# Two attentions: the first maxima turned earlier, later loads, and every row of maxima sent from ScalarE's queue

## The chip, the core and the metric

The program runs on one core of one Trainium2 chip. The metric is device time in microseconds (us) from the start to the end of one execution. The kernel before took 1791.27 us, the median of 3 runs (1789.46 to 1794.43). TensorE is called PE here, VectorE DVE, ScalarE ACT, GpSimd POOL, and SyncE, which only issues transfers, SP.

## The reference, cut to what matters

The program is a four-layer model on 16 sequences of 256 tokens, 128 features each. Each layer adds an attention-like part and an expert part to the residual. The change touches the attentions of the second layer (causal, called `att1`) and of the third (not causal, with low-rank additions, called `att2`). Both have 16 heads of 8 features:

```python
# layer 1 (causal)
q = proj(Wq, bq); k = proj(Wk, bk); v = proj(Wv, bv)            # 16 x 16 heads x 256 x 8
scores = einsum('bhqd,bhkd->bhqk', qc, k) * scale
scores = where(k_pos > q_pos, -inf, scores)
m = max(scores, axis=-1)
p = softmax(scores - m)
out = einsum('bhqk,bhkd->bhqd', p, v) @ Wo.T + bo
# layer 2 (not causal)
attn = softmax(einsum('bhnd,bhmd->bhnm', q, k) * ATTN_SCALE)
out = einsum('bhnm,bhmd->bhnd', attn, v) @ w_proj + b_proj
```

The time of these two attentions with the expert work that is set into the middle of each is about 720 to 1160 us and 1184 to 1530 us of the execution.

## The kernel before, in words

Both attentions are one function, `attention`. A projection stage (`projections`) computes all queries and keys, splits each into three bfloat16 parts and stores them to the chip's memory as `q_parts` and `k_parts`. Then a batch (one sequence) at a time is loaded back into one of four buffers of `qs` and `ks`, by 12 transfers that SP issues (`load_half` twice, L2149 and L2151). Load(b) means the 12 transfers of batch b. Batches 0 and 1 are loaded during the projection stage, batches 2 and 3 right after it.

The scores are computed twice. The first time (`maximum`, L2333) DVE takes the maximum of each row (`reduce`, L2515 and L2519). When the 8 pairs of heads of a batch are done, DVE splits the maxima into two bfloat16 parts (`split_maximum`), PE turns them (`turn_maximum`, L2416), ACT copies them to `mt` (L2497), and two small transfers (`top`, L2217, 8 KB each) put them as extra rows 48 and 49 into `qs`. Top(b) means the two transfers of batch b. The second time (`scores`, L2358) these rows subtract the maximum within the matmul, ACT takes the exponential (`exponent`, L2474), PE multiplies by the values (`values`, L2382), ACT copies the result out of the single bank O_BANK (`take_outputs`, L2479), and later steps turn, divide, turn back and project it.

The order is a loop over steps, `for step in steps`, written out for each engine: 8 steps to a batch, one for each pair of heads; the step within its batch is j. The maxima run LEAD = 12 steps ahead of the scores, so steps -12 to -1 hold only maxima. TURN = 5 places the turn and the copy of batch b + 1 in step j = 5 of batch b; project_values and the first `values` of the next pair of heads follow in step j = 6. On PE, the `values` of step 6 begin with a wait on `o_taken`, which counts the `take_outputs` of ACT; the one that it needs here is the first instruction of ACT in step 6, right behind the copy of the maxima in step 5:

```python
                    if k == 0:
                        ...
                        if gi >= 1:
                            pe.wait_ge(s.o_taken, gi)
```

Scores(8b) waits for top(b), maximum(8b) for load(b). At step MID (48 in att1, 32 in att2) all engines run the expert work (`job`) and then go on. In att2 that work has its own weights, `job.weights` (L2700 and L2695): six small transfers and two of 578 KB.

SP's order in the kernel before: the stores of the projection, load(2), then for each b from 0: top(b + 1), after b = 0 load(3), in att2 at b = 1 the weights, and load(b + 4) when the scores of batch b are done. Top(0) alone is issued by ACT.

Of the kernel before, what the change touches and what calls it, by code (L numbers as in the profile page):

```python
# [15 lines left out]
BATCH, T = 16, 256  # L16
# [2070 lines left out]
def attention(nc, g, title, prologue, project, wv, bv, wo, bo, q_parts, k_parts, causal, scale, moe=None, disp=None,  # L2087
              ybuf=None, r=None, dense=None):

    PAIRS = HEADS // 2  # L2090
    NP = BATCH * PAIRS
    NG = HEADS // 4
    LEAD = 12
# [6 lines left out]
    OT0, OT1, BACK, TURN, VALUES, OUT = 2, 3, 4, 5, 6, 7  # L2100
# [15 lines left out]
    with section(nc, title, *names, *PROJECT, "w_in", "filled", "ones_set", "consts", "biased", "qk_in0", "qk_in1", "qk_in2", "qk_in3",  # L2116
# [103 lines left out]
        with nc.Block() as block:  # L2220

            @block.sync
            def _(sp):
                def load(b):
                    if b % 2 == 0:
                        parts.chunk_stored(sp, b // 2)
                    for half in range(2):
                        load_half(sp, b, half)

                parts.sync(sp)  # L2230
                load(2)
                for b in range(BATCH - 1):
                    top(sp, b + 1)
                    if b == 0:
                        load(3)
                    if b == 1 and dense:
                        job.weights(sp)
                    if b + BUFS < BATCH:
                        sp.wait_ge(s.s_ready, (b + 1) * PAIRS)
                        load(b + BUFS)  # L2240
                    if moe and (b + 1) * PAIRS == MID:
                        job.first_tokens(sp)
                    if (moe or dense) and (b + 1) * PAIRS == MID:
                        job.sync(sp)
# [70 lines left out]
            def _(pe):  # L2315
# [121 lines left out]
                for step in steps:  # L2437
# [6 lines left out]
                        job.tensor(pe)  # L2444
                    if 0 <= step < NP:
                        scores(step)
                    if step + LEAD < NP:
                        maximum(step + LEAD)
                    if 2 <= step <= NP + 1:
# [2 lines left out]
                        turn_outputs(b - 1, j - OT0)  # L2452
                    if b >= 1 and j == BACK:
                        turn_back(b - 1)
                    if 0 <= b + 1 < BATCH and j == TURN:
                        turn_maximum(b + 1)
                    if 0 <= b + 1 < BATCH and j == VALUES:
                        project_values(b + 1)
# [4 lines left out]
            def _(act):  # L2463
# [17 lines left out]
                for step in steps:  # L2481
# [11 lines left out]
                    if 0 <= b + 1 < BATCH and j == TURN:  # L2493
                        act.wait_ge(s.turned_nm, b + 2)
                        if b >= 1:
                            act.wait_ge(mx_in[(b + 1) % 2], (b - 1) // 2 * 32 + 32)
                        nc.scalar.copy(mt[:, (b + 1) % 2, :], g.ps[0:4 * PAIRS, MISC, 0:T]).then_inc(s.mt_ready, 1)  # L2497
                        if b == -1:
                            top(act, 0)
                            parts.all_stored(act)  # L2500

            @block.vector
# [559 lines left out]
```

## Time and profile before

| what | value |
|---|---|
| median of 3 runs | 1791.27 us |
| time of the profiled execution | 1770.34 us |
| its span (first to last instruction) | 1768.5 us |
| PE, DVE, ACT, POOL busy | 84%, 71%, 53%, 45% of the span |
| granted clock of PE, mean | 0.927 |
| scores (L2358) of att1 | 760.57 us to 1153 us, with expert work from 843 to 1025 us |
| scores (L2358) of att2 | 1230.68 us to 1521 us, with expert work from 1294 to 1372 us |

The profiled execution took 1.84 us more than its span and was 20.9 us (1.2%) faster than the median. Busy shares are means over stages with different limits; what a stage is worth is read from its own stretch. In a row of windows the busy times stand in the order PE, PEld (weight loads), DVE, ACT, POOL, followed by PE's granted clock (1.00 is 2.4 GHz, 0.50 is 1.2 GHz), the busy share of the DMA engines and GB/s. In a timeline row the number in brackets is how long the engine sat idle before it and what ended that.

### The profile page before, as it was taken

What the parts mean: (1) busy time and instruction counts of PE and PEld (TensorE: products, weight loads), DVE (VectorE), ACT (ScalarE), POOL (GpSimd) and SP (SyncE); (2) the same over time, 40 slices, a digit from 0 to 9 for tenths busy, and PEclk for the clock granted to TensorE, in tenths of its full rate; (3) what the DMA queues carried; (4) which work ended last, traced back from release to release, by engine and by line L of the source; (5) the groups of instructions that cost most, each with busy time, mean ns of one, the idle gap of its engine ahead of it and who ended that gap; (6) DMA issues with size and microseconds to landing.
All of it is one profiled execution on the core that took longest, in us unless ns stands there. A gap on an engine that the chain in (4) does not pass through costs nothing. (4 is left out here: it accounts for less than half of the span.)

```text
span 1768.5 us, 31307 instructions
## 1 busy us (share of the span) xinstructions
PE 1479.8 (84%) x11180; PEld 921.1 (52%) x11180; DVE 1247.3 (71%) x2002; ACT 939.1 (53%) x1674; POOL 792.3 (45%) x722
## 2 busy tenths in 40 slices
PE   5993698898886877489799999954899999878997
PEld 5771244444342336256577766631345444566886
DVE  7745999999999987757355567668733899565335
ACT  1235578777775652546344456644554777533442
POOL 1477888778886743566144443124200000046341
PEclk9996899999999996779899999986899999779999
DMA  4522987877767946655322146207621342221223
GB/s 145 166 73 62 198 183 183 197 165 198 182 158 188 209 102 249 201 109 97 55 59 56 54 86 99 32 17 189 102 42 48 47 66 39 98 73 51 85 76 101
DMA packets 193559, 200.89 MB, mean 114 GB/s; under 512 B 22474, under 2 KB 142569, under 8 KB 193152
## 3 DMA queue, kind: packets, MB, share of 16 engines
q1 hardware_dynamic: 181816, 177.33, 42.9%
q0 software_dynamic: 11520, 21.52, 4.5%
q8 instruction: 93, 1.52, 0.4%
q14 instruction: 58, 0.48, 0.1%
q10 hardware_dynamic: 72, 0.03, 0.0%
HBM read 144.45 MB, written 57.48 MB: 114 GB/s over the span
## 5 line engine op out<-in xcount | busy, mean ns | idle before, releaser
L799 POOL TENSOR_TENSOR xn_t<-scan_b_rows,scan_du 128x1024 f32<-128x1024 f32 x128 | 303.9, 2381 | 94.2 <-DMA scan_b_rows<-states 62.5
L824 PE MATMUL banks<-scan_hc,ident 128*128 128x512 f32 x512 | 264.4, 629 | 77.4 <-DVE scan_hc L1006 76.7
L998 DVE TENSOR_TENSOR_SCAN banks<-banks,xn_t 128x1024 f32<-128x1024 f32 x128 | 293.1, 2290 | 27.9 <-POOL xn_t L799 17.7
L2474 ACT ACTIVATE att_pr<-banks 128x768 f32<-128x768 f32 (+1 forms) x256 | 234.4, 917 | 128.2 <-PE banks L2366 73.5
L824 PEld LDWEIGHTS banks<-scan_hc,ident 128*128 128x128 f32 x512 | 89.3, 194 | 212.5 <-DVE scan_hc L1006 147.1
L927 ACT ACTIVATE banks<-delta,scan_exp_centre,a_neg 128x510 f32<-128x510 f32 x256 | 189.3, 770 | 0.3
L2519 DVE TENSOR_REDUCE att_mb<-banks 128x4 f32<-128x1024 f32 x128 | 154.0, 1222 | 21.8 <-PE banks L2333 16.7
L2382 PE MATMUL banks<-att_pr,att_vx 128*32 128x256 f32 (+1 forms) x2048 | 155.7, 377 | 4.9 <-ACT att_ot L2479 3.3
L1006 DVE TENSOR_TENSOR scan_hc<-banks,scan_c_rows 128x1024 f32<-128x1024 f32 x128 | 156.5, 1223 | 3.8
L2515 DVE TENSOR_REDUCE att_mb<-banks 128x6 f32<-128x768 f32 x128 | 121.5, 956 | 46.8 <-PE banks L2340 45.7
L2333 PE MATMUL banks<-att_ks,att_qs 48*128 48x256 bf16 (+1 forms) x1024 | 112.4, 277 | 40.3 <-DMA att_ks<-k_parts 34.6
L1626 POOL IOTA xn_tok<- 128x32 int32 x1 | 0.2, 188 | 306.9 <-POOLq L78 306.9
L1442 POOL DMA_INDIRECT ybuf<-att_yo,att_xin x72 | 70.0, 972 | 126.0 <-DVE att_yo L1426 122.0
L2358 PE MATMUL banks<-att_qs,att_ks 50*128 50x256 bf16 (+1 forms) x1024 | 108.7, 269 | 15.3 <-DMA att_qs<-att_mt 12.7
L1342 PE MATMUL banks<-grouped_w,att_xt 128*128 x288 | 99.6, 469 | 0.4 <-DVE att_xt L1408 0.3
L925 ACT COPY banks<-zeros 128x4 f32<-128x4 f32 x128 | 20.8, 162 | 138.2 <-DVE scan_hc L1006 128.3
L1391 ACT ACTIVATE att_a<-banks 128x352 f32<-128x352 f32 x72 | 33.4, 464 | 107.0 <-PE banks L1342 107.0
L1061 POOL DMA_INDIRECT disp<-xn_tok,places x64 | 70.0, 1094 | 40.3 <-ACT u L545 24.9
L2298 POOL DMA_INDIRECT disp<-xn_tok,places x64 | 65.7, 1027 | 34.1 <-issue 12.4
L2333 PEld LDWEIGHTS banks<-att_ks,att_qs 48*128 48x128 bf16 x1024 | 48.7, 99 | 58.4 <-issue 24.7
L2358 PEld LDWEIGHTS banks<-att_qs,att_ks 50*128 50x128 bf16 x1024 | 39.8, 95 | 71.1 <-issue 39.9
L1408 DVE COPY att_xt<-banks 128x128 f32<-128x128 f32 x72 | 20.9, 292 | 76.3 <-PE banks L1332 76.3
(391 smaller groups left out, 3182.4 us busy)
## 6 DMA issues: line engine op xcount, KB each, us to landing
scan_b_rows<-states SPq DMA_DIRECT2D x128, 256.0 KB, 6.0
scan_c_rows<-states SPq DMA_DIRECT2D x128, 256.0 KB, 4.9
scan_ew<-f_packed SPq DMA_DIRECT2D x12, 578.0 KB, 6.0
q_parts<-att_p_parts SPq DMA_DIRECT2D x16, 384.0 KB, 3.6
k_parts<-att_p_parts SPq DMA_DIRECT2D x16, 384.0 KB, 5.6
att_qs<-q_parts SPq DMA_DIRECT2D x64, 96.0 KB
att_ks<-k_parts SPq DMA_DIRECT2D x64, 96.0 KB
disp<-blank_rows SPq DMA_DIRECT2D x1, 4680.0 KB, 15.1
```

Source lines behind the costliest of these rows:

```text
L799: nc.gpsimd.tensor_tensor(bu[:, q % AHEAD], b_rows[:, q % HELD, None, :].to_broadcast([P, DC, TT]), du[:, b % 2], ALU.mult).then_inc(s.bu_ ...
L824: nc.tensor.matmul(g.ps[:, Y0 + c, :], g.ident[:], hc[:, q % RING, c], start=False, stop=(q % DS == DS - 1)).then_inc(s.sum_done, 1)
L927: ins = nc.scalar.activation(inner(decays(q)[:, c]), inner(delta[:, c, span(b)]), ACT.Exp, scale=a_neg[:, c, n:n + 1], bias=exp_centre[:])
L998: v.tensor_tensor_scan(states, states, rows(bu[:, q % AHEAD]), 0.0, ALU.mult, ALU.add).then_inc(s.scan_done, 1)
L1006: v.tensor_tensor(hc[:, q % RING], decays(q), c_rows[:, q % HELD, None, :].to_broadcast([P, DC, TT]), ALU.mult).then_inc(s.hc_ready, 1)
L1342: ins = nc.tensor.matmul(g.ps[:, 4 * p + 1 + m, 0:H1], xt[:, p, :], rows(w13[:, bass.ds(expert[j], 1), m * H1:(m + 1) * H1]), start=True, ...
L2333: ins = nc.tensor.matmul(g.ps[:, 2 * m_slot(i) + half, lo:hi], qs[rows_of, p, j, q * P:(q + 1) * P], ks[rows_of, p, j, 0:hi - lo], start=T ...
L2358: ins = nc.tensor.matmul(g.ps[:, 2 * s_slot(i) + half, k * T:k * T + T - q0], ks[rows_of, p, j, k * P:(k + 1) * P], qs[rows_of, p, j, q0:T ...
L2382: ins = nc.tensor.matmul(g.ps[r * 32:(r + 1) * 32, O_BANK, q0:T], vx[:, b % 2, k, 4 * jg + r, :], pr[:, i % RING, half, k * T:k * T + T - q0],
L2474: nc.scalar.activation(pr[:, i % RING], g.ps[:, at:at + 2, 0:W], ACT.Exp, scale=scale).then_inc(s.p_ready, 1)
L2515: v.tensor_reduce(mb[:, b % 2, j, :].rearrange("p (g n) -> p g n", g=2), g.ps[:, at:at + 2, 0:W].rearrange("p g (n k) -> p g n k", k=P), A ...
L2519: v.tensor_reduce(mb[:, b % 2, j, :], g.ps[:, at:at + 2, :].rearrange("p g (n k) -> p (g n) k", k=T), AX_X, ALU.max).then_inc(s.m_taken, 1)
```

## The change

In `attention`, for both attentions: PE turns the maxima of batch 0 in step -4, before maximum(8), and no longer in step -3. SP waits until top(0) has landed before it issues load(2), and issues load(3) right behind it. The weights of att2's expert work are issued at b = 2, behind load(5), and no longer at b = 1, before load(5). Every top is now issued by ACT, directly after its copy of the maxima, where before SP issued all but the first.

```diff
                 parts.sync(sp)
+                sp.wait_ge(mx_in[0], 32)
                 load(2)
                 for b in range(BATCH - 1):
-                    top(sp, b + 1)
                     if b == 0:
                         load(3)
-                    if b == 1 and dense:
+                    if b == 2 and dense:
                         job.weights(sp)
                     if b + BUFS < BATCH:
                         sp.wait_ge(s.s_ready, (b + 1) * PAIRS)
                         load(b + BUFS)
...
                     if 0 <= step < NP:
                         scores(step)
+                    if step + LEAD == PAIRS:
+                        turn_maximum(0)
                     if step + LEAD < NP:
                         maximum(step + LEAD)
...
-                    if 0 <= b + 1 < BATCH and j == TURN:
+                    if 1 <= b + 1 < BATCH and j == TURN:
                         turn_maximum(b + 1)
...
                         nc.scalar.copy(mt[:, (b + 1) % 2, :], g.ps[0:4 * PAIRS, MISC, 0:T]).then_inc(s.mt_ready, 1)
+                        top(act, b + 1)
                         if b == -1:
-                            top(act, 0)
                             parts.all_stored(act)
```

`top` waits for the copy and issues two transfers:

```python
        def top(eng, b):
            eng.wait_ge(s.mt_ready, b + 1)
            for half in range(2):
                eng.dma_start(qs[half * HR + KR:half * HR + KM, b % BUFS],
                              mt[half * 2 * PAIRS:(half + 1) * 2 * PAIRS, b % 2, :]).then_inc(mx_in[b % 2], 16)
```

On ACT, att1, around the first top that ACT did not issue before (batch 1, step 5 of batch 0); att_pr is the exponential, att_mt the copy of the maxima, att_ot the copy of the outputs. Before:

```order
L2474 ACTIVATE att_pr<-banks 128x768
L2492 COPY att_on_t<-banks 128x256
L2474 ACTIVATE att_pr<-banks 128x768
L2497 CAST att_mt<-banks 32x256
L2479 COPY att_ot<-banks 128x256
L2474 ACTIVATE att_pr<-banks 128x768 x2
```

And now:

```order
L2476 ACTIVATE att_pr<-banks 128x768
L2494 COPY att_on_t<-banks 128x256
L2476 ACTIVATE att_pr<-banks 128x768
L2499 CAST att_mt<-banks 32x256
L2217 DMA att_qs<-att_mt 2x8x256 x2
L2481 COPY att_ot<-banks 128x256
L2476 ACTIVATE att_pr<-banks 128x768 x2
```

Two transfers now stand between the copy of the maxima and the copy of the outputs. The same holds in each of the 15 batches of each attention in which SP issued them.

On PE, start of att2: L2014 is the projection, L2333 the maxima, L2416 the turn, L2425 the values' projection.

```order
 L2014 MATMUL banks<-xn_t,att_p_w 128x512 x16
-L2333 MATMUL banks<-att_ks,att_qs 128x256 x40
+L2333 MATMUL banks<-att_ks,att_qs 128x256 x32
 L2416 MATMUL banks<-ident_b,att_m 32x128 x2
-L2333 MATMUL banks<-att_ks,att_qs 128x256 x4
+L2333 MATMUL banks<-att_ks,att_qs 128x256 x12
 L2425 MATMUL banks<-att_wv,xn_t 128x128 x2
```

The turn stands behind 8 maxima of 4 matmuls, no longer behind 10.

On SP, att2, around the weights (att_ln_g to att_fw). Before:

```order
L2151 DMA att_ks<-k_parts 8x8x256
L2217 DMA att_qs<-att_mt 2x8x256 x2
L2700 DMA att_ln_g<-f_g 128x1
L2700 DMA att_ln_b<-f_b 128x1
L2700 DMA att_aw<-f_aw 128x128
L2700 DMA att_nw<-f_nw 128x128
L2700 DMA att_ab<-f_ab 128x1
L2700 DMA att_nb<-f_nb 128x128
L2695 DMA att_fw<-f_packed 128x1029 x2
L2149 DMA att_qs<-q_parts 24x8x256
```

And now:

```order
L2151 DMA att_ks<-k_parts 8x8x256
L2702 DMA att_ln_g<-f_g 128x1
L2702 DMA att_ln_b<-f_b 128x1
L2702 DMA att_aw<-f_aw 128x128
L2702 DMA att_nw<-f_nw 128x128
L2702 DMA att_ab<-f_ab 128x1
L2702 DMA att_nb<-f_nb 128x128
L2697 DMA att_fw<-f_packed 128x1029 x2
L2149 DMA att_qs<-q_parts 24x8x256
```

The load ahead of the weights was load(4) and is now load(5); the load behind them was load(5) and is now load(6). The top is gone from SP's row.

## Rows read from the trace of the kernel before

**Rows 1.** Windows of PE's batches: us, busy us of each engine, granted clock, DMA share.

```profile
1064.70:1077.71 13.01, 13.01 (x277) 9.00 (x276) 10.00 (x18) 8.22 (x14) 4.26 (x6) 1.00 0.57 100
1437.56:1449.98 12.42, 12.29 (x149) 5.80 (x150) 11.72 (x17) 9.72 (x14) 0.00 (x0) 1.00 0.46 67
1437.56:1448.22 10.66, 10.53 (x129) 4.81 (x128) 10.20 (x15) 8.43 (x12) 0.00 (x0) 1.00 0.51 70
1077.71:1092.19 14.48, 13.02 (x277) 9.01 (x276) 11.54 (x19) 8.21 (x14) 4.22 (x6) 1.00 0.66 94
772.27:791.22 18.95, 15.80 (x282) 10.47 (x278) 10.42 (x18) 8.85 (x16) 12.51 (x20) 0.82 0.69 116
1243.53:1261.80 18.27, 15.01 (x149) 6.33 (x150) 11.97 (x16) 10.30 (x16) 5.53 (x10) 0.81 0.69 91
1261.80:1278.22 16.42, 12.36 (x149) 5.78 (x149) 12.25 (x18) 9.72 (x14) 0.00 (x0) 0.95 0.89 153
1278.22:1292.31 14.09, 13.97 (x129) 5.93 (x130) 9.88 (x13) 8.65 (x12) 0.00 (x0) 0.70 0.12 21
```

**Rows 2.** Timeline of att2 around a copy of the maxima: start, us, instruction.

```profile
1446.35 0.34 ACT L2497 CAST att_mt<-banks 32x256 bf16<-32x256 f32 x1
...
1446.60 0.36 ACT L2479 COPY att_ot<-banks 128x256 f32<-128x256 f32 x1
...
1447.01 0.64 PE L2382 MATMUL banks<-att_pr,att_vx 128*32 128x256 f32 x8
```

**Rows 3.** Timeline of att1 around a copy of the maxima.

```profile
800.70 0.36 ACT L2497 CAST att_mt<-banks 32x256 bf16<-32x256 f32 x1
...
800.97 0.36 ACT L2479 COPY att_ot<-banks 128x256 f32<-128x256 f32 x1
...
801.38 0.64 PE L2382 MATMUL banks<-att_pr,att_vx 128*32 128x256 f32 x8
```

**Rows 4.** Source line L2217, the tops issued by ACT: ns min/median/max, first and last start.

```profile
L2217 ACTq DMA_DIRECT2D att_qs<-att_mt x4: 621/636/1239, 753.3 to 1225.8; - x4
```

**Rows 5.** ACT's timeline: top(0) of att1 and of att2.

```profile
753.30 1.89 ACTq L2217 DMA_DIRECT2D att_qs<-att_mt  x2
...
1225.14 1.31 ACTq L2217 DMA_DIRECT2D att_qs<-att_mt  x2
```

**Rows 6.** PE's timeline, att1, in batch 10.

```profile
1086.79 0.44 PE L2406 MATMUL banks<-ident,att_on 128*128 128x128 f32 x2 [1.46 <-DVE att_on L2544]
```

**Rows 7.** PE's timeline, att1: scores(0), maximum(16), maximum(24).

```profile
760.57 0.39 PE L2358 MATMUL banks<-att_qs,att_ks 50*128 50x256 bf16 x2 [5.04 <-DMA att_qs<-att_mt]
...
766.60 0.23 PE L2333 MATMUL banks<-att_ks,att_qs 48*128 48x128 bf16 x2
...
782.12 0.29 PE L2333 MATMUL banks<-att_ks,att_qs 48*128 48x128 bf16 x2 [3.15 <-DMA att_ks<-k_parts]
```

**Rows 8.** PE's timeline, att2: maximum(16), maximum(24), scores(24).

```profile
1237.46 0.64 PE L2333 MATMUL banks<-att_ks,att_qs 48*128 48x256 bf16 x4
...
1253.05 0.61 PE L2333 MATMUL banks<-att_ks,att_qs 48*128 48x256 bf16 x4 [3.26 <-DMA att_ks<-k_parts]
...
1278.22 0.61 PE L2358 MATMUL banks<-att_qs,att_ks 50*128 50x256 bf16 x4 [3.94 <-DMA att_qs<-att_mt]
```

**Rows 9.** SP's timeline, att2: first transfer of load(3), and top(3).

```profile
1242.23 0.42 SPq L2149 DMA_DIRECT2D att_qs<-q_parts  x1
...
1270.95 1.27 SPq L2217 DMA_DIRECT2D att_qs<-att_mt  x2
```

**Rows 10.** DVE's timeline: end of the first split, att1, att2, and next maxima.

```profile
749.23 0.45 DVE L2534 TENSOR_TENSOR att_m<-att_m 128x32 bf16<-128x32 f32 x1
...
1224.05 0.21 DVE L2534 TENSOR_TENSOR att_m<-att_mb,att_m 128x32 bf16<-128x32 f32 x1
1224.18 3.47 DVE L2519 TENSOR_REDUCE att_mb<-banks 128x4 f32<-128x1024 f32 x3
...
1231.82 1.23 DVE L2519 TENSOR_REDUCE att_mb<-banks 128x4 f32<-128x1024 f32 x1 [1.55 <-PE banks L2333]
```

## The prediction, made before the changed kernel was run

> **What bounds the kernel now.** I read the windows by batch first. A batch of att1 takes 13.01 us with PE busy for all 13.01, and a batch of att2 takes 12.42 us with PE busy for 12.29, both at a granted clock of 1.00 [rows 1]. So in the steady stretches PE is the bound, and it runs its instructions in a fixed order: a wait of PE there has no later idle time in which to vanish. Batch 10 of att1 shows this. PE waits 1.46 us once [rows 6], and the batch takes 14.48 us, which is 13.02 us of PE work plus those 1.46, still at clock 1.00 [rows 1]. One wait of that size is paid in full, and nothing more is paid for the clock.
>
> Next I read PE's timeline for what it waits for. Three batches and a piece are longer than the steady ones, always behind a wait for a transfer: in att1 a wait of 3.15 us for load(3), in att2 3.26 us for load(3) and 3.94 us for top(3) [rows 7, 8]. The windows give what they cost in all: 18.95 instead of 13.01 us, 18.27 instead of 12.42, 16.42 instead of 12.42, and 14.09 instead of 10.66 for what follows top(3) [rows 1]. The granted clock of these stretches is 0.82, 0.81, 0.95 and 0.70: after each wait of over 3 us PE runs for a while at the lower of its two levels, 1.2 GHz, and that is why the cost is more than the wait. There is also the wait of 5.04 us for top(0) at the start of att1 [rows 7].
>
> **What the change can give back.** Load(3) is now issued right behind load(2), without waiting for top(1). In the trace load(3) takes 1253.05 - 1242.23 = 10.8 us from its first issue to the end of PE's wait in att2 [rows 8, 9]. Issued right behind load(2), it is there before PE asks. That gives 18.95 - 13.01 = 5.9 us in att1 and 18.27 - 12.42 = 5.9 us in att2.
>
> Top(3) of att2, issued at 1270.95, landed only for 1278.22 [rows 8, 9]: weights and load(5) were ahead of it. Load(5) now goes first, as soon as scores(15) is done, and the weights behind it. The same bytes stand ahead of top(3), but the load starts sooner, since SP does not issue top(2) and the weights before it, and PE asks 1.5 us later (below). I take the wait as almost gone: 4.0 + 3.4 us gained, 0.5 us left. If the order makes no difference, all 7.4 us stay lost; that end is in the range.
>
> The start of att1: the split ends at 749.68 [rows 10], so the turn is done there and no longer behind two maxima that wait for load(1). With 0.8 us for turn and copy, top(0) is issued at about 750.5 instead of 753.30 [rows 5], with no load(2) around it. The projection's last stores are still in flight then; I estimate 4.5 us until it lands, so scores(0) can start near 755 instead of 760.57 [rows 7]. But load(2) now starts only when top(0) has landed. With the 10.8 us of load(3) it arrives at about 765.8, and maximum(16), which needs it, ran at 766.60 before [rows 7]. So 5 us of gain shrink to 0.8 us. Then top(1) goes out while load(3) is still in flight, where before it went out on a quiet queue; I charge 0.5 us.
>
> The start of att2: the split ends only at 1224.26 [rows 10], when PE had its maxima 8 and 9 done already, so the earlier turn brings nothing there. It even takes the two maxima from DVE, whose three reductions of 1.16 us started right behind the split [rows 10]; DVE is 1.2 us later. That eats what a faster top(0) gives, because before DVE had 1.55 us of idle time at 1231.82, and the third scores wait for that reduction in both orders. Load(2) starts about 3 us after top(0) was issued at 1225.14 [rows 5], at 1228, and lands at 1238.8, against 1237.46 for maximum(16) [rows 8]: a loss of 1.3 us, and 0.2 us for top(1) behind load(3). Both starts together, without ACT's share: +0.3 and -1.5, so -1.2 us.
>
> Sum of all this: 5.9 + 5.9 + 7.4 - 0.5 - 1.2 = 17.5 us gained.
>
> **What ACT's issuing costs.** Thirty tops, 15 in each attention, move from SP to ACT. Two transfers take ACT 1.31 us when nothing else is being issued and took 1.89 us while SP was issuing load(2) [rows 5]; one is 636 ns in the median [rows 4]. In the steady stretch of att2 the copy of the maxima starts at 1446.35 and ends at 1446.69. Before, the copy of the outputs followed at 1446.60, ended at 1446.96, and PE started the values that need it at 1447.01 [rows 2]. There is no slack between these two. In att1 it is the same: 800.97 + 0.36 = 801.33, and PE starts at 801.38 [rows 3]. Now ACT waits for its copy to end (1446.69), issues for 1.31 us with 0.04 us around it, and comes to the copy of the outputs at 1448.06 instead of 1446.60: 1.46 us later. PE's values wait by as much, and behind them in PE's order stand the projection of the values, the next scores and the next maxima, for which DVE and ACT wait. By the batch with the 1.46 us wait [rows 1, 6] nothing of it comes back. 30 x 1.46 = 43.8 us.
>
> The trace never shows ACT computing directly behind a transfer, so the price has two ends. If the issue does not hold up the next instruction, it is 0. If every pair costs 1.89 us as in the start of att1, it is 30 x 2.04 = 61 us. I take 1.46 us, since in the steady stretch SP is not issuing loads at that moment. The tops of batches 1 may be a little dearer for that reason.
>
> A page of the Trainium skill makes the small end imaginable. DMA: Bandwidth & Descriptors, in its section on the anatomy of one DMA, puts the dispatch by a sequencer at about 50 ns; 60 transfers would then be 3 us, and the sum would turn into a gain of over 14 us. The section is about transfers from POOL, and rows 4 show 636 ns on ACT's queue. Perfetto Trace Analysis, in its section on the HWDGE DMA instruction, says that the sequencer is free for the next instruction only when the profiled interval of the transfer ends, and that the descriptor generator is shared and locked; by that rule the whole 1.31 us stand in ACT's way, and the 1.89 us beside SP's issues fit it. I follow the second.
>
> **The sum.** 43.8 - 17.5 = 26.3 us slower: 1770.34 + 26.3 = 1796.6 us for the profiled execution. The median of the runs is 1791.27, 20.9 us above that execution, so the same difference on the median gives 1817.6 us, 1.5% more. A difference of 0.3%, about 5.4 us, is what a measurement of this kernel can tell from none.
>
> **Rivals.**
> ACT's issues hide (10%). The sequencer runs ahead or ACT's compute goes on beside it, and only the gains remain: 1791.3 - 17.5 = 1773.8 us, faster. For it speaks only that no row shows ACT computing behind a transfer; against it, ACT's two transfers took 1.31 us one behind the other and SP's two of top(3) 1.27 us, twice the 636 ns of one [rows 4, 5, 9].
> Half of it is hidden (8%). If only one of the two issues is in the way (0.65 + 0.1 us, 22 us in all), the sum is +5, about 1796 us, between no change and slightly slower. For it speaks that the bank of the outputs could be read while a second issue is under way; against it, ACT's copies and exponentials start in program order in all rows.
> The transfers collide anew (17%). Load(2), load(3) and top(1) now stand in one row, and load(5), the weights and top(3) in another. If top(1) waits over 3 us behind load(3), PE falls to 1.2 GHz again and the 5.9 us of a batch are lost where they were gained; if top(3) still waits for the weights, 7.4 us are lost. For it speak top(0)'s 1.89 us issue beside load(2) and its wait of 5.04 us; against it, that PE asks for each top 1.5 us later than before. With both: 1817.6 + 13 = 1831 us, slower too. It decides from the point where a top lands more than about 4 us after its issue.
> The forecast itself has 65%.
>
> **Range and chances.** Within the forecast, the price of a top may be 1.35 to 1.6 us (40 to 48 us) and the gains 10 to 22 us, so 1809 to 1829 (1791.3 + 40 - 22 and 1791.3 + 48 - 10). To hold 8 in 10 the range reaches down to the half-hidden case and up to the collision: 1797 to 1832 us. Slower by over 0.3%: forecast, collision and a bit less than half of the half-hidden case, 85%; within 0.3%: 4%; faster: 11%.
>
> **What the profile after would show.** Each steady batch of att1 at about 14.5 us and of att2 at about 13.9 us, at clock 1.00, with PE's L2382 waiting about 1.4 us for the copy of the outputs once in each batch, and ACT's row of L2217 with 64 transfers of 620 to 640 ns, none by SP. Scores(0) of att1 near 755 us if nothing before it moves, a wait for load(2) at maximum(16), and no wait of over 3 us at maximum(24) in either attention. The forecast is wrong if the steady batches keep 13.0 and 12.4 us; then the issues are hidden. If they lengthen by much more than 1.5 us, a second wait or the lower clock joined in. If the steady batches are as forecast and the sum is not, the error is in the starts.

## The result and the profile after

The changed kernel is slower, by more than was forecast.

| | kernel before | changed kernel |
|---|---|---|
| first comparison, median us | 1790.37 (4 runs) | 1833.03 (4 runs, 1825.53 to 1843.83) |
| ratio, 95% interval | | 1.0267 [1.0231, 1.0304] |
| second comparison, median us | 1790.76 (28 runs) | 1832.15 (4 runs, 1821.83 to 1839.18) |
| ratio, 95% interval | | 1.0250 [1.0204, 1.0297] |
| profiled execution, span us | 1768.5 | 1829.6 |
| granted clock over the span | 0.927 | 0.917 |

Forecast were 1817.6 us and at most 1832; the ratio was to be 1.0147. By the two ratios the change costs 45 to 48 us instead of 26.3. The two spans differ by 61 us, but those must not be set against each other: the profiled execution of before ran in a surrounding that is 20 us quicker (shown below, with run e10). The steps are therefore judged by single batches and by the ratios. Of all executions in this document one, of run e7, ran slow (2283.86 us at a granted clock of 0.60); it is left out of that run's ratio.

Windows by batch of the changed kernel, columns as in [rows 1]. The first two are steady batches of att1 and att2, then batches 11 and 12 of att2, batch 14 of att1, the starts (batches 0 and 1 of att1, batches 0, 1 and 2 of att2), and last batch 4 of att2, the first behind the expert work.

```profile
1091.80:1106.27 14.47, 13.09 (x278) 9.01 (x278) 10.07 (x19) 8.33 (x14) 4.25 (x6) 1.00 0.58 95
1484.96:1498.84 13.88, 12.30 (x151) 5.80 (x150) 11.73 (x17) 9.83 (x14) 0.00 (x0) 1.00 0.39 61
1512.71:1527.57 14.86, 13.25 (x149) 6.24 (x150) 11.86 (x17) 9.94 (x14) 0.00 (x0) 0.93 0.42 69
1527.57:1543.22 15.65, 14.08 (x149) 6.39 (x148) 11.66 (x16) 9.94 (x14) 0.00 (x0) 0.85 0.32 36
1165.93:1181.38 15.45, 13.12 (x229) 8.39 (x229) 6.42 (x15) 8.18 (x14) 0.68 (x1) 0.89 0.01 2
757.51:777.44 19.93, 14.90 (x251) 9.63 (x248) 9.07 (x14) 7.27 (x11) 14.48 (x20) 0.66 0.66 116
777.44:795.75 18.31, 15.34 (x280) 10.44 (x277) 10.50 (x18) 8.83 (x16) 12.88 (x21) 0.88 0.44 89
1267.33:1286.60 19.27, 15.44 (x119) 5.63 (x120) 12.68 (x18) 9.20 (x11) 16.70 (x29) 0.50 0.68 84
1286.60:1300.47 13.87, 12.29 (x153) 5.80 (x150) 11.64 (x16) 10.10 (x15) 1.87 (x4) 1.00 0.45 61
1300.47:1315.18 14.71, 12.36 (x149) 5.80 (x149) 12.26 (x18) 9.83 (x14) 0.00 (x0) 1.00 0.76 151
1409.91:1429.24 19.33, 16.32 (x149) 7.14 (x150) 12.22 (x16) 11.89 (x16) 0.00 (x0) 0.75 0.06 17
```

Read the first two against [rows 1]: 13.01 became 14.47 and 12.42 became 13.88, 1.46 us each, with PE's busy time the same within 0.1 us and the clock at 1.00. That is the forecast to the hundredth. Then read the next two: PE runs the same 149 instructions in 13.25 and 14.08 us instead of 12.30, at a clock of 0.93 and 0.85. PE's idle time in them is that of the steady batch (1.61 and 1.57 us against 1.58), so what they take longer goes with the clock, and in the kernel before no batch from 5 to 14 of att2 had a clock under 1.00. Batch 4 of att2 is the dearest of its kind: 19.33 us at 0.75. The same batch of the kernel before, in its second profile (run e0), takes 15.31 us at 0.89:

```profile
1367.68:1382.99 15.31, 13.74 (x148) 6.30 (x148) 11.92 (x16) 11.56 (x16) 0.00 (x0) 0.89 0.03 7
```

Of the 4.0 us between them 1.46 are the pause. Batches 0 and 1 of att1 have a low clock too (0.66 and 0.88), and batch 1 takes 18.31 us instead of the 14.5 that the forecast implies; in run e4, with a pause nearly as long, it takes 14.61, so this is not in every execution.

ACT's timeline in the steady stretch of att2, answering to [rows 2] and [rows 5]:

```profile
1493.75 0.35 ACT L2499 CAST att_mt<-banks 32x256 bf16<-32x256 f32 x1
1494.12 1.28 ACTq L2217 DMA_DIRECT2D att_qs<-att_mt  x2
1495.44 0.37 ACT L2481 COPY att_ot<-banks 128x256 f32<-128x256 f32 x1 [1.35 <-issue]
```

and PE's behind it:

```profile
1495.87 0.64 PE L2382 MATMUL banks<-att_pr,att_vx 128*32 128x256 f32 x8 [1.57 <-ACT att_ot L2481]
```

The copy of the outputs starts 0.04 us after the second issue ends (1494.12 + 1.28 = 1495.40), where before it started before the copy of the maxima had ended. "Issue" is the profile's word for time in which ACT waited for nothing that it can show: its sequencer was taken. PE's next values wait for that copy. Top(0) of att1, answering to [rows 5]:

```profile
754.18 1.91 ACTq L2217 DMA_DIRECT2D att_qs<-att_mt  x2
```

It takes 1.91 us although SP now issues nothing between 750.3 and 757.5 us. The source line of the tops, answering to [rows 4]:

```profile
L2217 ACTq DMA_DIRECT2D att_qs<-att_mt x64: 620/621/1244, 754.2 to 1566.9; - x64
```

The waits for transfers in the starts, answering to [rows 7, 8]: maximum(16) of att1 and, in the second fence, the first turn, scores(0) and maximum(16) of att2, then scores(24).

```profile
768.88 0.29 PE L2333 MATMUL banks<-att_ks,att_qs 48*128 48x128 bf16 x2 [2.24 <-DMA att_ks<-k_parts]
```

```profile
1262.71 0.40 PE L2416 MATMUL banks<-ident_b,att_m 128*32 128x128 bf16 x2 [4.20 <-DVE att_m L2536]
...
1267.33 0.61 PE L2358 MATMUL banks<-att_qs,att_ks 50*128 50x256 bf16 x4 [1.14 <-DVE att_mb L2521]
...
1276.61 0.61 PE L2333 MATMUL banks<-att_ks,att_qs 48*128 48x256 bf16 x4 [0.93 <-DMA att_ks<-k_parts]
...
1315.18 0.39 PE L2358 MATMUL banks<-att_qs,att_ks 50*128 50x256 bf16 x4 [0.77 <-DMA att_qs<-att_mt]
```

Maximum(24) waits for nothing any more in either attention, and top(3) of att2 makes PE wait 0.77 us instead of 3.94. In their place stand waits for load(2) and, in att2, 4.20 us of PE for DVE's split, which it used to spend on maxima 8 and 9.

### The profile page after: what moved, and what is told of

It reads as the page before. It is cut to its first block and busy times, and to the rows that moved or that the text cites. A ratio compares the mean times of both kernels' runs of the same rounds, so it can differ in the third digit from the quotient of the medians.

```text
span 1829.6 us, 31309 instructions
## 1 busy us (share of the span) xinstructions
PE 1503.6 (82%) x11180; PEld 930.6 (51%) x11180; DVE 1245.6 (68%) x2002; ACT 942.8 (52%) x1674; POOL 796.1 (44%) x722
## 5 line engine op out<-in xcount | busy, mean ns | idle before, releaser
L2382 PE MATMUL banks<-att_pr,att_vx 128*32 128x256 f32 (+1 forms) x2048 | 159.9, 386 | 50.1 <-ACT att_ot L2481 48.6
L2333 PE MATMUL banks<-att_ks,att_qs 48*128 48x256 bf16 (+1 forms) x1024 | 114.6, 281 | 34.5 <-DMA att_ks<-k_parts 27.1
L2382 PEld LDWEIGHTS banks<-att_pr,att_vx 128*32 128x32 f32 x2048 | 42.2, 111 | 93.7 <-ACT att_ot L2481 56.0
L1391 ACT ACTIVATE att_a<-banks 128x352 f32<-128x352 f32 x72 | 33.3, 463 | 106.5 <-PE banks L1342 106.5
L2333 PEld LDWEIGHTS banks<-att_ks,att_qs 48*128 48x128 bf16 x1024 | 50.1, 101 | 53.0 <-issue 27.3
L2481 ACT COPY att_ot<-banks 128x256 f32<-128x256 f32 x128 | 47.5, 371 | 55.2 <-issue 41.2
```

Of the source, the lines that this page charges most:

```text
L2333: ins = nc.tensor.matmul(g.ps[:, 2 * m_slot(i) + half, lo:hi], qs[rows_of, p, j, q * P:(q + 1) * P], ks[rows_of, p, j, 0:hi - lo], start=T ...
L2382: ins = nc.tensor.matmul(g.ps[r * 32:(r + 1) * 32, O_BANK, q0:T], vx[:, b % 2, k, 4 * jg + r, :], pr[:, i % RING, half, k * T:k * T + T - q0],
```

## The experiments

Times are medians; a ratio is that to the kernel before in the same comparison. Runs e0 to e3 were made together, e4 to e7 together, and e8 to e11 together. Each group ran on a chip of its own, and the kernel before took 1771.0, 1766.0 and 1790.8 us in these three. So runs of different groups are compared by their ratios. A difference of two ratios is given in us of 1771, unless said. An account by batches rests on one profiled execution of each kernel.

### e0: the kernel before once more

No edit.

> The kernel before, unchanged, for a second profiled execution. The first one (1770.3 us) was 17 to 24 us shorter than all other executions of it. Theory A (ACT's issues explain all that is lost): the profile again shows no wait for something remote in att1 and a time near 1770. Rival B (the profiled execution was a lucky one, and part of the excess over the forecast is not the change's): a time near 1790, with waits of 1 to 2.5 us for something remote on DVE and ACT in the first half of att1, where the changed kernel shows nine of them, and batches 2 to 7 of att1 longer than 13.02 us.

Measured: 1770.61 us, ratio 1.0000 [0.9975, 1.0025]. Its profile has none of the waits for something remote, so theory A's sign is there; batches 2 to 4 of att1 take 13.1 to 13.6 us. But the kernel before took 1771 us here and 1790 in the first comparison, so neither theory is settled by this run; e8 and e10 do that. The run shows one thing more. Windows of batches 1 and 2 of att2:

```profile
1245.59:1264.06 18.47, 15.10 (x150) 6.40 (x150) 12.00 (x16) 10.28 (x16) 4.37 (x8) 0.82 0.70 91
1264.06:1276.49 12.43, 12.30 (x150) 5.79 (x150) 11.74 (x17) 9.72 (x14) 0.00 (x0) 1.00 0.81 165
```

Batch 1, which waits for load(3), is as long as in [rows 1]. Batch 2, which waited 3.94 us for top(3) there, takes 12.43 us here: that wait is not in every execution.

### e1: SP issues the tops again

```diff
                     if b == 0:
                         load(3)
+                    top(sp, b + 1)
                     if b == 2 and dense:
...
-                        top(act, b + 1)
                         if b == -1:
+                            top(act, 0)
```

> The changed kernel, but SP issues the tops of batches 1 to 15 again (that of batch 1 behind load(3)); ACT issues only top(0). Steady batches go back to 13.0 and 12.4 us in every theory. Theory A (all of the excess comes with ACT's issues, through the one wait per batch and the lower clock behind it): the changed kernel minus about 65 us, 17 us under the kernel before, near 1773. Rival B (ACT's issues cost the forecast's 43.8 us, the other 17 to 21 us come from the new order of the loads): near 1790, no gain over before. Rival C (the gains of 17.5 us were not there): also near 1790, but with batches of 18 to 19 us still in both starts.

Measured: 1759.86 us, ratio 0.9956 [0.9933, 0.9979], 7.8 us under before by the ratio and 11.1 by the medians. From the changed kernel's 1.0250 and 1.0267 to 0.9956 is 52 to 55 us, so ACT's issues cost more than the forecast's 43.8: rival B falls, its even with before is outside the interval. The gain is smaller than the 17 us of theory A. Rival C falls too: batch 1 takes 13.02 us in att1 and 12.42 in att2.

### e2: nothing but ACT's issues

```diff
                 for b in range(BATCH - 1):
-                    top(sp, b + 1)
                     if b == 0:
+                        sp.wait_ge(mx_in[1], 32)
                         load(3)
...
                         nc.scalar.copy(mt[:, (b + 1) % 2, :], ...)
+                        top(act, b + 1)
                         if b == -1:
-                            top(act, 0)
```

> The kernel before, but every top is issued by ACT's queue; load(3) on SP waits for top(1)'s landing, as it stood behind top(1) before. Early turn, later load(2) and later weights are left out. Theory A: +60 to +65 us on the kernel before, about 1853. Rival B: +43.8, about 1834. Steady batches 14.47 and 13.87 us in both; a difference would be in the batches of att1 up to 7 and in the clock of the stretches.

The added wait lets SP issue load(3) only when top(1) has landed, a little later than before, when it stood behind top(1)'s issue. It costs little: the two batches 1 are 0.2 and 0.4 us longer than in e0 beside the pause.

Measured: 1822.33 us, ratio 1.0297 [1.0257, 1.0337], so 52.6 us [45.5, 59.7]. This is more than 43.8 and less than theory A's 60. It agrees with the 52 to 55 us of the opposite edit in e1, so the cost does not depend on the new order of the loads. Windows of att2's batches 9 to 14:

```profile
1474.95:1488.82 13.87, 12.29 (x151) 5.79 (x150) 11.72 (x17) 9.83 (x14) 0.00 (x0) 1.00 0.43 61
1488.82:1503.62 14.80, 13.22 (x149) 6.21 (x149) 11.84 (x17) 9.94 (x14) 0.00 (x0) 0.93 0.44 67
1503.62:1519.56 15.94, 14.33 (x150) 6.61 (x150) 11.79 (x16) 9.84 (x14) 0.00 (x0) 0.85 0.31 46
1519.56:1534.38 14.82, 13.24 (x149) 6.25 (x149) 11.75 (x16) 9.94 (x14) 0.00 (x0) 0.93 0.36 44
1534.38:1550.28 15.90, 14.31 (x151) 6.61 (x150) 11.79 (x16) 9.84 (x14) 0.00 (x0) 0.85 0.01 3
1550.28:1564.66 14.38, 12.05 (x133) 5.49 (x133) 6.99 (x12) 9.83 (x14) 0.00 (x0) 0.94 0.00 1
```

Every one of these batches has the same wait of 1.57 to 1.60 us for the copy of the outputs (2.10 in the last). In some the clock stays at 1.00 and in others it falls to 0.85. A batch at 0.93 costs 0.93 us more than one at 1.00, a batch at 0.85 costs 2.0 to 2.1 us more. DMA is at 46 GB/s and under in four of the five low ones, so no burst of transfers is needed for it.

### e3: ACT issues one step later

```diff
+                    if 0 <= b < BATCH - 1 and j == TURN + 1:
+                        top(act, b + 1)
                     if 0 <= b + 1 < BATCH and j == TURN:
...
-                        top(act, b + 1)
                         if b == -1:
+                            top(act, 0)
```

> The changed kernel, but ACT issues the tops of batches 1 to 15 one step later, behind that step's exponential and no longer between the copy of the maxima and the copy of the outputs. If the loss is where the issue stands and not that ACT issues, a batch pays only what ACT has no slack for behind that exponential: 0 to 0.7 us for each of 30 tops. Theory A: 1770 to 1795 us. Rival: the issue costs 1.46 us wherever it stands in ACT's stream, since an exponential behind it comes as late as the copy did: near 1833 and steady batches still at 14.47 and 13.87 us.

Measured: 1763.67 us, ratio 0.9966 [0.9941, 0.9991], steady batches 13.02 and 12.42 us. The rival falls. The time can't be told from that of e1. ACT's timeline in the steady stretch of att2:

```profile
1421.74 0.35 ACT L2501 CAST att_mt<-banks 32x256 bf16<-32x256 f32 x1
1421.99 0.36 ACT L2481 COPY att_ot<-banks 128x256 f32<-128x256 f32 x1
1422.11 0.62 ACTq L2217 DMA_DIRECT2D att_qs<-att_mt  x1
1422.25 1.02 ACT L2476 ACTIVATE att_pr<-banks 128x1024 f32<-128x1024 f32 x1
1422.77 0.62 ACTq L2217 DMA_DIRECT2D att_qs<-att_mt  x1
1424.05 1.02 ACT L2476 ACTIVATE att_pr<-banks 128x1024 f32<-128x1024 f32 x1 [0.78 <-PE banks L2358]
```

Here ACT's compute and its issues run side by side. The first issue starts at 1422.11, when the copy of the maxima has just ended, although in program order it stands behind the copy of the outputs, which still runs, and the exponential, which starts later. It seems that both were handed to the engine already; the profile does not show that step. The issues end at 1423.39, and the next instruction behind them, the exponential at 1424.05, has to wait for PE anyway. An issue holds back what stands behind it in the program, not what stands ahead of it. The Trainium skill, Perfetto Trace Analysis, in its section on the DVE / Act engine instruction, has the sequencer push a compute instruction into a wait queue and then turn to the next one; the trace agrees: the issue at 1422.11 starts before the exponential at 1422.25.

### e4: the same pause without a transfer

```diff
                         nc.scalar.copy(mt[:, (b + 1) % 2, :], ...)
+                        if b >= 0:
+                            nc.scalar.copy(idle[:], g.ident[:, 0:1].to_broadcast([P, IDLE]))
```

IDLE is 1536, the target is a buffer of its own, and all else is run e1.

> The kernel of run e1 (SP issues the tops), with a copy of 128x1536 elements on ACT behind each copy of the maxima but the first, estimated at 1.46 us from ACT's 370 ns for 256 and 1024 ns for 1024 elements: the same pause at the same place, with no transfer issued by ACT. Theory A (a pause of that length in each batch lets PE's clock fall now and then, and that is the excess over 30 x 1.46): e1 (1759.9) + 43.8 + 7 to 15, so 1811 to 1819, and a granted clock under 1.00 in some batches, most likely the last ones of both attentions. Rival B (the excess comes with the transfers on ACT's queue, which collide with something): e1 + 43.8 = 1804, every steady batch at 14.47 and 13.87 us and clock 1.00.

Measured: 1804.43 us, ratio 1.0235 [1.0199, 1.0271]. ACT's timeline in att2, and three windows, batches 11 to 13 of att2:

```profile
1494.26 0.35 ACT L2502 CAST att_mt<-banks 32x256 bf16<-32x256 f32 x1
1494.51 1.46 ACT L2504 CAST att_idle<-ident 128x1536 bf16<-128x1536 f32 x1
1495.88 0.36 ACT L2484 COPY att_ot<-banks 128x256 f32<-128x256 f32 x1
```

```profile
1485.47:1499.26 13.79, 12.29 (x149) 5.80 (x149) 11.72 (x17) 11.09 (x15) 0.00 (x0) 1.00 0.38 60
1499.26:1513.97 14.71, 13.21 (x149) 6.22 (x149) 11.86 (x17) 11.20 (x15) 0.00 (x0) 0.93 0.37 51
1513.97:1529.81 15.84, 14.34 (x150) 6.62 (x150) 11.79 (x16) 11.10 (x15) 0.00 (x0) 0.85 0.01 2
```

The pause came out at 1.37 us (13.79 - 12.42, and 14.39 - 13.02), 30 x 1.37 = 41.1 us. From e1 to e4 the ratios differ by 0.0279, 49 us; against e5 and e6, made together with e4, it is 50 to 51. So 8 to 10 us come on top, with an uncertainty about as large (e4's four executions take 1797.6 to 1815.3 us). That something comes on top is shown by the windows: the clock falls in two of these batches behind a pure pause of ACT, with SP issuing the tops. Rival B, every steady batch at clock 1.00, falls by them. Its time (1804) was met, but by 41 + 8 and not by 44 + 0; theory A's 1811 to 1819 was missed, since the pause came out shorter and the kernel before was 5 us quicker here.

### e5: load(2) at once

```diff
                 parts.sync(sp)
-                sp.wait_ge(mx_in[0], 32)
                 load(2)
```

In run e1.

> Run e1 without SP's wait for top(0) before load(2). Theory A (the wait only moves the time: what scores(0) gains, maximum(16) and batch 0 lose): the same time as e1 within 2 us in each start, scores(0) 4 to 5 us later, batch 0 5 us shorter. Rival (the early top is worth what scores(0) shows): 4 to 8 us slower than e1. In att2 before and e1 stand 32.3 and 33.0 us from the first maximum to batch 1's first scores, in att1 31.8 and 32.7, so I expect A.

Measured: 1755.98 us, ratio 0.9946 [0.9927, 0.9965], the same as e1 within both intervals. In att1 scores(0) come 17.65 us after the first maximum instead of 14.68 in e1, and batch 0 takes 11.69 instead of 17.98 us. From the first maximum to the first scores of batch 1 it is 29.3 us against 32.7 in e1 and 31.8 in e0. In att2 the three are 33.3, 33.0 and 32.3. The wait for top(0) moves the time and saves none; in att1 the loss that it brings looks larger than I expected, but the ratios can't confirm that.

### e6: the first turn in its old place

```diff
-                    if step + LEAD == PAIRS:
-                        turn_maximum(0)
...
-                    if 1 <= b + 1 < BATCH and j == TURN:
+                    if 0 <= b + 1 < BATCH and j == TURN:
```

In run e1.

> Run e1 with the first turn of the maxima back in its old place, behind maxima 8 and 9. Forecast of the steps: att1 up to 0.8 us slower or no change, since the split's end lets the turn run at about the same time; att2 about 1.2 us faster, since DVE gets its reductions of maxima 8 and 9 right behind the split again. Together within 2 us of e1.

Measured: 1757.81 us, ratio 0.9951 [0.9935, 0.9967], the same as e1. The turn's place is worth nothing that can be measured. The single starts do not answer to the steps: in att2 the first scores of batch 1 come 33.5 us after the first maximum, no better than e1's 33.0. In att1 they come 38.0 us after it, against 32.7, because in this profile top(1), issued by SP at 769.65 behind load(3), landed only for 778.03:

```profile
778.03 0.40 PE L2359 MATMUL banks<-att_qs,att_ks 50*128 50x256 bf16 x2 [5.06 <-DMA att_qs<-att_mt]
```

That is the collision which the prediction's third rival describes. The other profiles with load(3) ahead of top(1) have at most 0.6 us of it in att1. Whether it is in every execution of e6 is not known: the six take 1754.6 to 1760.2 us, and the profiled one is the second longest (1759.3).

### e7: the dense weights at batch 1

```diff
-                    if b == 2 and dense:
+                    if b == 1 and dense:
```

In run e1.

> Run e1 with the dense weights issued at batch 1 again. Theory A (the wait of 3.94 us for top(3) was a matter of that one profiled execution; the second profile of before does not show it): the same time as e1 within 2 us. Rival B (the recorded step: later weights are worth 7.4 us): 7 us slower than e1, with a wait for top(3) in att2.

Measured: 1763.80 us, ratio 0.9982 [0.9966, 0.9999], 0.26% or 4.6 us over e1, and 5.5 to 6.4 us over e6 and e5, which were made together with it. The profile has a wait for top(3) of 1.38 us. By the last two theory A falls: the later weights are worth something, 5 to 6 us, and rival B's 7 can't be excluded. The profile holds one thing that this edit can't have made, since it touches att2 alone. Batch 10 of att1 answers to [rows 1, 6], where the recorded rule was read:

```profile
1078.27:1094.26 15.99, 14.53 (x278) 9.90 (x278) 11.54 (x19) 8.32 (x14) 4.22 (x6) 0.89 0.61 84
```

and PE's timeline in it:

```profile
1087.35 0.44 PE L2407 MATMUL banks<-ident,att_on 128*128 128x128 f32 x2 [1.46 <-DVE att_on L2547]
```

The same wait of 1.46 us, and this time the clock is 0.89 and the batch 1.51 us longer than the 14.48 of [rows 1]. Nine profiles are of kernels without ACT's pause; this is the one of the nine in which batch 10 has a low clock.

### e8: the changed kernel once more

No edit.

> The changed kernel, unchanged, for a second profiled execution. Theory A (ACT's pause in each batch, and the lower clock that it brings in some batches): 2.2 to 3.0% over the kernel before, steady batches 14.47 and 13.87 us, some later batch of each attention with a clock under 1.00, and batches 2 to 5 of att1 near 14.6 us as in run e2. Rival B (the change itself brings the waits for something remote that the first profiled execution shows in the first half of att1): they are there again and those batches take 16.8 to 18.5 us.

Measured: 1832.15 us, ratio 1.0250 [1.0204, 1.0297]. Steady batches at 14.47 and 13.87 us, and again batches of att2 with a low clock, among them 10 and 11:

```profile
1490.14:1504.97 14.83, 13.24 (x149) 6.26 (x149) 11.86 (x17) 9.94 (x14) 0.00 (x0) 0.93 0.43 69
1504.97:1520.66 15.69, 14.08 (x150) 6.41 (x150) 11.67 (x16) 9.94 (x14) 0.00 (x0) 0.85 0.31 42
```

The waits for something remote are there too (14 of them in att1), and its batches 2 to 4 take 16.8 to 19.2 us, as rival B said. What they belong to, e10 tells.

### e9: half of each top by ACT

```diff
-        def top(eng, b):
+        def top(eng, b, halves=(0, 1)):
...
-            for half in range(2):
+            for half in halves:
...
                         load(3)
+                    top(sp, b + 1, (1,))
...
-                        top(act, b + 1)
+                        top(act, b + 1, (0,) if b >= 0 else (0, 1))
```

> The changed kernel, but of the two transfers of a top ACT issues only the first and SP the second (top(0) stays on ACT as a whole). If a transfer on ACT's queue costs what the profile says it lasts, the pause is 0.64 + 0.1 us and a batch 13.75 and 13.15 us: 30 x 0.73 = 22 us over run e1. Theory A (the lower clock comes with the length of the pause): an excess over that of 0 to 4 us, under that of run e4. Rival (two engines issue at the same moment and hold each other up, as 1.89 us for top(0) beside load(2) in the kernel before): each transfer takes up to 0.95 us and a batch up to 14.0 and 13.4 us, 30 us over e1.

Measured: 1803.96 us, ratio 1.0072 [1.0047, 1.0098], 1.16% over e1, 20.8 us of 1791, with about 6 us of uncertainty. ACT's timeline and SP's at the same moment, then the windows of batches 11 of att2 and 8 and 10 of att1:

```profile
1459.99 0.62 ACTq L2217 DMA_DIRECT2D att_qs<-att_mt  x1
1460.66 0.37 ACT L2482 COPY att_ot<-banks 128x256 f32<-128x256 f32 x1 [0.69 <-ACT att_mt L2500]
```

```profile
1459.99 0.62 SPq L2217 DMA_DIRECT2D att_qs<-att_mt  x1
```

```profile
1490.48:1503.70 13.22, 12.29 (x150) 5.80 (x150) 11.73 (x17) 9.84 (x14) 0.00 (x0) 1.00 0.44 62
...
1077.67:1091.49 13.82, 13.09 (x277) 9.01 (x277) 10.08 (x19) 8.33 (x14) 4.27 (x6) 1.00 0.70 99
...
1105.31:1122.87 17.56, 15.80 (x277) 10.67 (x276) 11.60 (x19) 8.42 (x14) 4.21 (x6) 0.81 0.61 88
```

A batch costs 0.80 us more, 30 x 0.80 = 24 us, and in att2 all ten batches from 5 on keep the clock at 1.00. Over all nothing is measured on top of the pauses. One batch pays all the same: batch 10 of att1, which has the 1.46 us wait beside the pause, takes 17.56 us at 0.81 where 13.82 + 1.46 = 15.28 were due. The rival falls: SP and ACT issue at the same moment and the transfer on ACT still takes 0.62 us.

### e10: only load(3) ahead of top(1)

```diff
                 for b in range(BATCH - 1):
-                    top(sp, b + 1)
                     if b == 0:
                         load(3)
+                    top(sp, b + 1)
```

> The kernel before, with load(3) issued ahead of top(1) and nothing else. Theory A (this one step holds the whole gain of the changed kernel's order): batch 1 at 13.02 us in att1 and 12.42 us in att2, 5.35 and 6.05 us less than in the second profile of before, so 8 to 12 us faster than before, as run e5. Rival (without the early turn and the later weights a wait moves to top(1) or top(3)): 3 to 7 us faster, with a wait for att_mt of over 1 us.

Measured: 1787.00 us, ratio 0.9981 [0.9956, 1.0005], 3.4 us by the ratio and not told from nothing. Batch 1 of att2 is at 12.42 us, but scores(24) wait again, between theory A and the rival:

```profile
1292.13 0.39 PE L2358 MATMUL banks<-att_qs,att_ks 50*128 50x256 bf16 x4 [1.69 <-DMA att_qs<-att_mt]
```

The run settles what e0 and e8 left open. The order of issue is that of before but for one load, no top is issued by ACT, and yet att1 up to the expert work has 16 waits of this kind, here two on DVE and ACT:

```profile
822.22 0.96 DVE L2515 TENSOR_REDUCE att_mb<-banks 128x6 f32<-128x768 f32 x1 [1.96 <-remote]
829.87 0.81 ACT L2474 ACTIVATE att_pr<-banks 128x768 f32<-128x768 f32 x1 [1.50 <-remote]
```

All four profiles of this comparison (before at 1790.8 us) have them, 14 to 21 each; none of the eight of the comparisons in which before took 1766 to 1771 us (e0 to e7) has one, nor has the first profile of before. The changed kernel's first profile, of the comparison in which before took 1790 us, has 11. So they belong to where or when the kernels ran, not to the change; chip and time can't be told apart here, since each group of runs had one chip.

### e11: load(3) ahead of top(1), and the weights later

```diff
-                    if b == 1 and dense:
+                    if b == 2 and dense:
```

In run e10.

> As run e10, with the dense weights issued at batch 2 as in the changed kernel. Run e7 lost 0.26% when they came earlier, with a wait of 1.38 us for top(3), so 1.4 to 4 us faster than e10, 9 to 13 us faster than before. If the weights' place is without effect, the same time as e10 within 1 us.

Measured: 1782.16 us, ratio 0.9959 [0.9933, 0.9986], 7.3 us under before and 0.22%, 3.9 us, under e10, which is no more than the uncertainty of that difference. There is no wait for top(3) in its profile, and att2's batches 1 and 2 take 12.42 us each. By the ratios this is as much as the whole new order gains in e1 (0.9956), with two moved lines, and no early turn, wait for top(0) or ACT queue.

Best of all by the median and the ratio is e5, 0.9946 [0.9927, 0.9965], which beats both kernels; e1, e3, e5, e6 and e11 can't be told apart.

## Why the prediction was wrong

**The step that failed** is "nothing more is paid for the clock" and "by the batch with the 1.46 us wait nothing of it comes back. 30 x 1.46 = 43.8 us". The pause itself was right in place and size. But the rule was read from one batch, with one wait, in one execution. What the pause does when it comes in every batch stands in the clocks of 18 batches in each profile, 7 to 14 of att1 and 5 to 14 of att2. The last column is how much longer the 18 take than in e0, beyond 18 pauses:

| kernels | pause per batch | batches of 18 at clock 0.98 or less | beyond the pauses, us |
|---|---|---|---|
| before (two profiles), e1, e3, e5, e6, e10, e11 | none | 0 in each | 0.4 at most |
| e7 | none | 1 (batch 10 of att1) | 1.5 |
| e9 | 0.80 us | 1 (batch 10 of att1) | 2.4 |
| e4 | 1.37 us | 3 | 4.3 |
| changed kernel, e8, e2 | 1.46 us | 5, 7, 6 | 5.4, 8.3, 8.9 |

Of e2's 8.9 us, 8.6 stand in its six low batches. Batch 4 of att2, outside the 18, adds up to 2.6 us in the changed kernel. Which batches they are differs between executions of the same kernel; what decides it was not found. In sum ACT's issues cost 52.6 us (e2, interval 45.5 to 59.7), or 52 to 55 by undoing them (e1), instead of 43.8: about 9 us too little in the term (2 to 16 by e2's interval). With no transfer on ACT an excess of that size is there (e4, about 8 us), and at 0.80 us per batch none is measured (e9, 20.8 us for 24 us of pauses). The times alone would hardly part these; that it is the lower clock is shown by the windows, PE taking 13.2 to 14.3 us for what it does in 12.3. The Trainium skill, TensorE: Matmul & The Clock Gate, in its section on a second failure mode, tells of a kernel whose frequent micro-idles of PE let the clock swing between its two levels, against a single change in another; e2 and e4 agree in kind. I had not weighed it, and it would have pointed the right way.

**The gains were the second miss**: 7.8 us by the ratio of e1 (interval 3.7 to 11.9) and 11.1 by its medians, instead of 17.5. Point by point:
- Load(3), 5.9 + 5.9 us: right. Batch 1 takes 13.02 and 12.42 us in e1.
- The starts, -1.2 us: about right. From the first maximum to the first scores of batch 2 it is 45.7 us in att1 and 45.5 in att2 in e1, against 50.2 and 50.8 in e0, so 4.5 + 5.3 = 9.8 us for starts and load(3) together, where 10.6 stood. Scores(0) of att1 were to start near 755 and started at 757.51, but the first maximum was 3.2 us later too (743.72 against 740.52). The wait for load(2) came as said, 2.24 us in the changed kernel, though it is 5.16 us in e1.
- In att2 "the earlier turn brings nothing": right as far as e6 can tell, whose time is that of e1.
- Top(3) and the weights, 6.9 us: probably too large. Pairs of runs give 4.6 us (e7 to e1), 5.5 and 6.4 us (e7 to e6 and e5) and 3.9 us (e10 to e11), with 3 to 5 us of uncertainty each. The 3.94 us wait and the low clock behind it were in one execution of before and not in the other (e0).
- These parts add up to 14 us or more, and e1 shows 8 to 11. The rest was not found; it is about as large as the uncertainties together. One thing that can eat gains is the late top(1) of e6, which the forecast charged with 0.5 us.

The account by ratios is 52.6 - 7.8 = +44.8 us of 1771, 2.5%, as the changed kernel has (2.50 and 2.67%). The forecast was 43.8 - 17.5. Both terms erred to the same side, and by about the same amount: 8.8 us too little cost and 9.7 us too much gain.

**The rivals.** "ACT's issues hide" was wrong for this place in the program, and true one step later (e3). The reason that the rival gave, that the sequencer runs ahead, holds in one direction only: the issue passes compute that stands ahead of it, and holds up what stands behind it, which in e3 waits for PE anyway. "Half hidden" did not occur, since both issues are in the way (1.28 us and e9's 0.62). "The transfers collide anew" did not occur in the changed kernel's profiles: top(1) made no wait, top(3) one of 0.77 us. It occurred in one profile with the same row of loads (e6, 5.06 us for top(1)). Its time (1831) was nearly met by luck, with another cause. That the skill's rule on the sequencer (Perfetto Trace Analysis, section on the HWDGE DMA instruction) was to be followed, and not the small dispatch of DMA: Bandwidth & Descriptors, is confirmed: the copy starts 0.04 us after the issue ends. But the 1.89 us of att1's top(0), which the prediction put down to SP's issuing beside it and from which it took the dear end of the price, do not come from it: with SP silent they are 1.91 us, and in e9 one transfer by ACT beside one by SP takes 0.62. What makes this first pair slow was not found.

**The conversion from profile to median** held as a ratio. The 20.9 us between the profiled execution of before and its median were not the profiler's: the kernel before takes 1771 us in one surrounding and 1791 in the other, and the profile, by its time and by having none of the waits for something remote, came from the quicker one.

## What to carry to other kernels

A transfer issued by a compute engine costs that engine the issue's whole length only for what stands behind it in the program; put it in front of an instruction that waits for another engine anyway, not between two that run back to back. When the busiest engine gets the same short pause in every iteration, look at its granted clock over many iterations and executions before writing "pause times count": here 0.80 us per batch cost in sum no more than itself, and 1.37 to 1.46 us cost about a fifth more by the medians. A wait that stands in a single profile is worth what it costs times how often it occurs; take a second profile of the kernel before ahead of pricing its removal.

## What the runs showed of the hardware that was not expected

- PE's granted clock fell in 3 to 7 of 18 batches in each profile with a pause of 1.37 or 1.46 us in every batch. With 0.80 us it fell in one (e9), which has a 1.46 us wait beside the pause. Without the pause it fell in one batch of one profile of nine, behind that wait alone (e7). Which batches it is differs between profiles.
- ACT's issue at 1422.11 in e3 started beside one compute instruction of its own engine that stands ahead of it in the program (1421.99 to 1422.35) and before another one that does (1422.25).
- The same kernel takes 1766 to 1771 us in some comparisons and 1790 in others, and the profiles of the latter show waits of DVE and ACT for something remote, up to 4.1 us each, in att1's first half. What they wait for was not found.
- The first two transfers that ACT issues in att1 take 1.89 us with SP issuing beside them (kernel before) and 1.91 us with SP silent (changed kernel); a steady pair takes 1.28. Why was not found.
- Top(1) of att1, two transfers of 8 KB, was waited for until 8.4 us after its issue in e6, where it stood behind a load, and in the other profiles with that order PE waited 0.6 us at most for it in att1.
